# A four-layer attention and expert kernel: first tile ahead of the output folding, two more narrow-expert buffers, an early fold

## The chip, the cores and the metric

The kernel runs on one core of a Trainium2 chip. The metric is device microseconds (us) of one execution, median over runs. Matrix products run on TensorE (PE; its weight loads are shown as PEld), elementwise work on VectorE (DVE) and ScalarE (ACT), indexed transfers and a few powers on GpSimd (POOL). SyncE (SP) issues most of the transfers (DMAs). Each engine runs its own list of instructions in order and waits on semaphores.

## The reference

`x` is a (2, 1024, 256) fp32 tensor and `ctx` holds 77 keys a batch. Four layers follow each other, each a cross attention and a feed-forward block, each with layernorm and a residual sum:

```python
# layer 0 attention, 16 heads of 64 on 16-wide slices of the input, 77 keys, key mask
scores = einsum('bhqe,bhke->bhqk', Q, K) / 8
attn = softmax(where(mask, -1e9, scores))
out = einsum('bhqk,bhkv->bqhv', attn, V).reshape(Bq, Sq, -1) @ Wo.T + bo
# layer 0 feed-forward: 64 experts of hidden width 192, 8 of them a token, at most 128 rows an expert
x_buf = zeros((E * C + 1, 256)).at[idx].set(x[tok])
h = silu(einsum('ecd,edf->ecf', xb, w_gate)) * einsum('ecd,edf->ecf', xb, w_up)
y = einsum('ecf,efd->ecd', h, w_down)          # weighted, summed by token, plus a shared expert
# layer 2 feed-forward: 8 experts of width 1024 with gelu, 2 a token; layer 3 attention: 16 heads, 77 keys
```

Layer 1 (a second attention and a local attention with its feed-forward) and the last expert block are not touched.

## The kernel before, in words

The stages run one after the other: `a0` (first attention), `m0` (narrow experts), `a1`, local attention, `a2`, `m2` (`halved_experts`, the third block), `a3` (`fourth_attention`), `m3`. A stage's buffers are opened in its own scope; what must outlive a stage, or be there ahead of it, sits in an `Ahead` object.

**First attention, `low_rank_attention` (L796).** Tokens are taken in 16 tiles of 128. Because there are only 77 keys, the query weights are multiplied into the keys ahead of the tiles (`fold`, 16 small products, each copied out), and the output weights are multiplied into the value weights (`wp`). The function `outputs` (L1320) does the latter: 8 fp32 products give one bias row (`rows_made`, L1324), 8 more give `wp` in two halves (`wp_made`, L1327); DVE's `split_bo` adds `bo`, splits the row into three bf16 parts, and copies `wp` out (`wp_copied`). The parts go to DRAM and come back as three rows `bo3`, which each `project` adds by a bf16 product with ones. Then, for every tile: `turn` (transpose the normalised tile), `score` in three groups, DVE's `mask` and `maximum`, ACT's exponential, `turn_p` (transpose the probabilities, 10 pieces), `value`, DVE's `invert` and `unload`, `turn_o`, `project`, DVE's `add`, which gives the new `x` of the tile; then its router logits, its ranks among experts, and its slots (`place_slot`, L1136).

The order on each engine is written out by hand as cycles: in cycle c, PE does `turn_p(c)`, `turn(c+2)`, `score(c+1)`, `value(c)`, `turn_o(c)`, `project(c)`, and DVE works on add(c-1), mask(c+1), norm(c+3), invert(c) and so on. Cycle −1 is the start: the scores of tile 0, and behind them `outputs`. The layernorm statistics of the tiles (`stats_pair`, two tiles a pair) are spread over the first cycles by `STAT_PAIRS`; in a cycle they stand behind `norm` and ahead of `invert`. POOL raises the variances of a pair to the power −1/2 (`power_x`), and of each new tile, and scatters the rows of a tile to the experts' slots: 8 indirect DMAs a tile, 128 in all (L941), 7 a cycle and the rest at the end.

SP loads the inputs, then fills the slots with zeros in 16 transfers, half of them ahead of its wait for the split bias row and half behind; then the shared expert's weights, zeros for the sums, the first four gate-and-up weights, and, when every scatter is done, the first row loads.

**Narrow experts, `narrow_experts` (L2359).** 32 pairs of experts. Buffers: four for rows (`xb`), four for gate-and-up weights (`wgu`, 768 KB a pair), six for down weights (`wd`, 384 KB). SP's loop issues, for each pair q from 4 on, the rows, which wait until pair q−4's rows are transposed (`turned`) and its row numbers found (`found`), then the gate-and-up and the down weights, each when its buffer is free:

```python
for q in range(NG):
    load_d(q)
for q in range(NG, npair):
    load_x(q)
    load_gu(q)
    load_d(q)
```

**Third block, `halved_experts` (L2798).** 16 passes (two an expert). `every_step` runs phases with lags: on PE the row transposition and first product of a pass, then its second product (`down`) one step later and the back-transposition of the result (`back`, in two parts) two steps later; DVE copies it out weighted (`copy_y`), POOL scatter-adds it to the sums (L2846).

**Fourth attention, `fourth_attention` (L323).** SP loads the first tiles of `x`, the first batch's fold (1,232 KB), the bias parts `c3` and the values, once the stage has begun.

## Time and profile before

| | |
|---|---|
| time, median of 3 runs | 2244.62 us (2235.33 to 2250.46) |
| the profiled execution: its own time, its span | 2244.4 us, 2242.6 us |
| mean granted PE clock | 0.951 |
| busy share: PE, PEld, DVE, ACT, POOL | 91%, 68%, 49%, 42%, 27% |
| DMA over the span | 255.35 MB, mean 114 GB/s |
| narrow experts: PE's first instruction | 257.30 |
| fourth attention: SP's first load | 1737.52 |

The rows are of one profiled execution, times in us from the start of the span. A timeline line is a run of like instructions on one engine: its start, the us they took, the code line, output and input by the program's names, shapes, and how many (x10). In brackets stands the idle time of that engine just ahead of it and what ended it. SPq is SP's DMA issue. The clock is a share of full speed: 1.00 is 2.4 GHz, 0.50 is 1.2 GHz.

### The profile page before, as it was taken

Reading aid. Unit: us, or ns where it says so; the run is one execution under the profiler, and the core shown is the slowest. Engines: PE = TensorE matmul, PEld = TensorE weight load, DVE = VectorE, ACT = ScalarE, POOL = GpSimd, SP = SyncE. Lnnn points to the kernel's source line nnn. Section 1 sums busy time; section 2 is a strip of 40 time slices with the busy share of each in tenths; the row PEclk is TensorE's granted clock in tenths of the full one; section 3 lists DMA queues with packets and bytes.
Section 4 is the critical chain, followed back from the end, with each engine's and each line's share of the span. In section 5 each row is a group of like instructions: output and inputs, shape, how many; then the busy total and the mean of one; then the engine's idle time right before and its main releaser. Section 6 shows DMA issues by size and latency. Waiting matters only on the chain. (4 is left out here: it accounts for less than half of the span.)

```text
span 2242.6 us, 39355 instructions
## 1 busy us (share of the span) xinstructions
PE 2048.1 (91%) x12889; PEld 1530.6 (68%) x12889; DVE 1099.0 (49%) x4126; ACT 935.7 (42%) x2965; POOL 614.7 (27%) x553
## 2 busy tenths in 40 slices
PE   7999899785999899799989979879998899699999
PEld 4676577563666555466655568768886577599998
DVE  4776244475777632577754358721221565411221
ACT  3565122253777521377752135422222566333332
POOL 0677466421222100122210002222223122212212
PEclk9999899887999999999999979989999999799999
DMA  7600599875900110100000091111121910466662
GB/s 280 251 17 30 164 341 342 237 278 169 374 14 11 39 33 0 40 11 11 11 11 0 1 332 43 41 43 28 35 34 15 302 39 35 152 196 175 183 183 56
DMA packets 162510, 255.35 MB, mean 114 GB/s; under 512 B 37484, under 2 KB 125967, under 8 KB 161270
## 3 DMA queue, kind: packets, MB, share of 16 engines
q1 hardware_dynamic: 132886, 224.62, 28.7%
q0 software_dynamic: 29424, 28.21, 7.1%
q8 instruction: 107, 1.75, 0.3%
q14 instruction: 93, 0.76, 0.1%
HBM read 165.95 MB, written 101.04 MB: 119 GB/s over the span
## 5 line engine op out<-in xcount | busy, mean ns | idle before, releaser
L2752 ACT ACTIVATE m3e_ht<-m3e_h_bank,m3w_b 128x128 f32<-128x128 f32 x312 | 88.9, 368 | 191.9 <-PE m3e_h_bank L2724 191.9
L3360 ACT ACTIVATE la_probs<-la_probs,la_nb,la_invnorm 128x256 f32<-128x256 f32 x256 | 150.2, 594 | 0.0
L2735 PE MATMUL m3e_y_bank<-m3w_w,m3e_ht 128*128 x624 | 141.0, 380 | 0.0
L941 POOL DMA_INDIRECT m_xbuf<-m0w_rows,m0w_slots x128 | 127.2, 993 | 40.3 <-issue 36.9
L2906 ACT ACTIVATE m2e_ht<-m2e_h_bank,m2w_b 128x270 f32<-128x270 f32 x128 | 62.2, 486 | 179.3 <-PE m2e_h_bank L2871 179.2
L2699 POOL DMA_INDIRECT out<-m3e_y,m3e_dest x39 | 60.4, 1548 | 238.2 <-DVE m3e_y L2787 224.3
L2735 PEld LDWEIGHTS m3e_y_bank<-m3w_w,m3e_ht 128*128 128x128 f32 x624 | 115.8, 190 | 14.0
L2846 POOL DMA_INDIRECT m_sum<-m2e_y,m2e_dest x48 | 70.2, 1462 | 197.7 <-DVE m2e_y L2954 187.0
L2764 DVE COPY m3e_xt<-m3e_turned_bank 128x256 f32<-128x256 f32 x39 | 16.6, 425 | 217.1 <-PE m3e_turned_bank L2712 217.1
L2871 PE MATMUL m2e_h_bank<-m2e_xt,m2w_w 128*128 128x270 f32 x512 | 121.7, 396 | 0.0
L2443 POOL DMA_INDIRECT m_sum<-m0e_y,m0e_dest x64 | 98.8, 1544 | 82.6 <-DVE m0e_y L2615 57.1
L2881 PE MATMUL m2e_y_bank<-m2e_ht,m2w_w 128*128 128x270 f32 x512 | 119.2, 391 | 0.0
L2871 PEld LDWEIGHTS m2e_h_bank<-m2e_xt,m2w_w 128*128 128x128 f32 x512 | 97.2, 192 | 19.0
L3190 POOL COPY la_spread<-la_inv 128x512 f32<-128x512 f32 x32 | 19.5, 610 | 325.6 <-DVE la_inv L3282 325.6
L2881 PEld LDWEIGHTS m2e_y_bank<-m2e_ht,m2w_w 128*128 128x128 f32 x512 | 96.1, 190 | 18.2
L3185 POOL TENSOR_TENSOR la_invnorm<-la_clamped,all_minushalf 128x16 f32<-128x16 f32 x32 | 92.8, 2901 | 36.4 <-DVE la_clamped L3254 36.4
L3271 DVE CUSTOM_DVE_ANT_0 la_probs<-la_score_bank,lo_shut 128x256 f32<-128x256 f32 x256 | 98.0, 420 | 6.7 <-PE la_score_bank L3456 6.6
L2468 PE MATMUL m0e_gu_bank<-m0e_xt,m0w_wgu 128*128 128x128 f32 x768 | 93.2, 279 | 0.0
L2724 PE MATMUL m3e_h_bank<-m3e_xt,m3w_w 128*128 128x128 f32 x768 | 91.0, 278 | 0.2 <-DVE m3e_xt L2764 0.2
L2468 PEld LDWEIGHTS m0e_gu_bank<-m0e_xt,m0w_wgu 128*128 128x128 f32 x768 | 90.4, 196 | 0.6 <-issue 0.6
L2724 PEld LDWEIGHTS m3e_h_bank<-m3e_xt,m3w_w 128*128 128x128 f32 x768 | 88.9, 194 | 0.6 <-DVE m3e_xt L2764 0.6
L3647 PE MATMUL lf_g_bank<-lf_zt,lo_w 128*128 128x512 f32 x160 | 79.6, 622 | 7.7 <-DVEq L3565 7.7
(505 smaller groups left out, 4767.0 us busy)
## 6 DMA issues: line engine op xcount, KB each, us to landing
m3w_w<-in_m_w SPq DMA_DIRECT2D x32, 1024.0 KB, 6.6
m0w_wgu<-in_m_gu SPq DMA_DIRECT2D x32, 768.0 KB, 10.2
m_xbuf<-all_zeros SPq DMA_DIRECT2D x38, 528.0 KB, 5.9
m2w_w<-in_m_w SPq DMA_DIRECT2D x16, 1024.0 KB, 12.4
m3e_w<-in_m_w SPq DMA_DIRECT2D x15, 1024.0 KB, 5.9
m0e_wd<-in_m_down SPq DMA_DIRECT2D x32, 384.0 KB, 11.2
m_xbuf<-all_zeros SPq DMA_DIRECT2D x16, 576.0 KB, 7.3
m0w_xb<-m_xbuf SPq DMA_DIRECT2D x32, 288.0 KB, 8.0
```

Of the source, the lines that this page charges most:

```text
L941: nc.gpsimd.indirect_dma_start(k.slot_buffers[m.name][0][:, :], bass.IndirectOffsetOnAxis(ahead.slots[:, t, i:i + 1], 0), ahead.rows[t % R ...
L2443: nc.gpsimd.indirect_dma_start(sums[j][:, :], bass.IndirectOffsetOnAxis(dest[q % NY][:, i:i + 1], 0), y[q % NY][:, i, :], None, bounds_che ...
L2468: last = nc.tensor.matmul(gu_ps[u][:, i * 512 + j * P:i * 512 + (j + 1) * P], wgu[q % NG][:, i * DC + c, j * P:(j + 1) * P], xt[u][:, c, i ...
L2724: last = nc.tensor.matmul(h_ps[t % 2][half][:, i * R:(i + 1) * R], w1[t % NW][:, c, f0:f0 + P], xt[t % 2][:, c, :], start=c == 0, stop=c = ...
L2735: last = nc.tensor.matmul(y_ps[t % 2][0:R, 0:D], h_t[t % 2][:, c, :], ahead.w2[:, bass.ts(e, 1), c, :].rearrange("p o f -> p (o f)"), star ...
L2752: last = nc.scalar.activation(h_t[t % 2][:, 4 * half + i, :], h_ps[t % 2][half][:, i * R:(i + 1) * R], m.act, bias=ahead.b1[:, bass.ds(e * ...
L2871: last = nc.tensor.matmul(h_ps[n % 3][:, 0:N], ahead.w1[:, h // 2, c, f * P:(f + 1) * P], xt[h % 2][:, c, :], start=c == 0, stop=c == DC - 1)
L2881: last = nc.tensor.matmul(y_ps[c][:, 0:N], ahead.w2[:, h // 2, f, c * P:(c + 1) * P], h_t[h % 2][:, f, :], start=f == 0, stop=f == HC - 1)
L3185: nc.gpsimd.tensor_tensor(inv_norm[t % 2][:, :], clamped[t % 2][:, :], k.minus_half[:, :], ALU.pow).then_inc(powered.sem, 1)
L3271: last = nc.vector.tensor_tensor_reduce(probs[u][:, hh, :], score_ps[j][:, i * 2 * P:(i + 1) * 2 * P], lo.shut[:, int(t % TB == 0), :], 1. ...
L3360: last = nc.scalar.activation(probs[u][:, hh, :], probs[u][:, hh, :], ACT.Exp, bias=nb[u][:, hh:hh + 1], scale=inv_norm[u][:, hh:hh + 1], ...
L3647: last = nc.tensor.matmul(ps[:, :], w1[:, dc, i, :], z_t[g % 2][:, dc, :], start=dc == 0, stop=dc == DC - 1)
```

## The change

- **First attention.** PE's `outputs` is cut into `output_row` and `output_fold`. They leave cycle −1: in cycle 0, the row comes behind `turn_p(0)` and the fold behind `score(1, 0)`. The fold uses the first of the three `pt` banks and waits until its earlier content has been copied; `turn_p(1)` and `project(0)` wait for the fold's copy. On DVE, the row's and the fold's copies are steps of cycle 0, and the split of the row comes at the end of it. `project` of tiles 0 and 1 adds the bias by one fp32 row instead of the three bf16 rows. The statistics stand ahead of `mask` in their cycle, and one pair moves from cycle 1 to cycle 2. SP issues all 16 zero fills ahead of its wait for the split row.
- **Narrow experts.** `wgu` has six buffers: the last two lie in the memory of the first attention's `fold` and `values`. `wd` becomes lasting, and the first attention's weights (`wo`, `wq`, `wv`, `wk`, `bq`) lie in its memory. During the first attention, SP waits until those weights are used up and loads six down weights; it loads gate-and-up 4 after the last score and 5 after the last values product. The stage's own loop then loads only rows for pairs 4 and 5, and rows and weights from pair 6.
- **Third block and fourth attention.** The first fold and `c3` get buffers of their own, loaded by SP at the end of the third block's loads. In its last step, the second part of `back(14)` goes into the middle of `down(15)`, and DVE's copy of it ahead of `evict(15)`.

The diff, cut (the new fold's uses in `fourth_attention` are left out):

```diff
@@ -228,8 +228,14 @@
+            gu = 2 * DC * 2 * m.hidden
+            self.under = [s.sb("under0", [P, 16 * B * J]), s.sb("under1", [P, B * len(PROB_CHUNKS) * WIDE])]
             self.wgu = [s.sb(f"wgu{i}", [P, 2 * DC, 2 * m.hidden]) for i in range(4)]
+            self.wgu += [u[:, 0:gu].rearrange("p (c f) -> p c f", c=2 * DC) for u in self.under]
             self.wgu_in = s.lasting_sems("wguin", len(self.wgu))
+            self.down = s.sb("down", [P, 6, 3, D])
+            self.wd = [self.down[:, i, :, :] for i in range(6)]
+            self.wd_in = s.lasting_sems("wdin", len(self.wd))
@@ -266,6 +272,10 @@
+    def load_down(self, sp, q):
+        n = len(self.wd)
+        sp.dma_start(self.wd[q % n], self.d["down"][q]).then_inc(self.wd_in[q % n], 16)
@@ -298,6 +308,22 @@
+class FoldAhead:
+    def __init__(self, k):
...
+        s = Scope(k, self.ctx, "a3w")
+        self.fold = self.ctx.enter_context(k.nc.sbuf_tensor("a3w_fold0", [P, 16, DC, J], F32, side="right"))
+        self.c3 = self.ctx.enter_context(k.nc.sbuf_tensor("a3w_c3", [3, D], BF16, side="right"))
+        self.fold_in, self.c3_in = s.lasting_sems("in")
+    def load(self, sp, src):
+        sp.dma_start(self.fold[:, :, :, :], src.fold[:, 0]).then_inc(self.fold_in, 16)
+        sp.dma_start(self.c3[:, :], src.parts).then_inc(self.c3_in, 16)
@@ -334,7 +360,7 @@
         s = Scope(k, ctx, "a3")
-        fold, vw, c3 = s.sb("fold", [P, B, 16, DC, J]), s.sb("vw", [P, B, NC, D]), s.sb("c3", [3, D], BF16)
+        fold, vw, c3 = [k.fold_ahead.fold, s.sb("fold1", [P, 16, DC, J])], s.sb("vw", [P, B, NC, D]), k.fold_ahead.c3
@@ -381,9 +407,6 @@
-                def load_fold(b):
-                    sp.dma_start(fold[:, b, :, :, :], src.fold[:, b]).then_inc(fold_in[b], 16)
                 def load_vw(b):
@@ -391,13 +414,11 @@
                     sp.dma_start(k.x[:, t, :], k.m2_sum[t * P:(t + 1) * P, :]).then_inc(sem, 16)
-                load_fold(0)
                 load_x(1)
-                sp.dma_start(c3[:, :], src.parts).then_inc(c3_in, 16)
                 load_vw(0)
                     load_x(p)
-                load_fold(1)
+                sp.dma_start(fold[1][:, :, :, :], src.fold[:, 1]).then_inc(fold_in[1], 16)
                 ahead.load_router(sp)
@@ -790,7 +812,7 @@
 PER_CYCLE = 7
-STAT_PAIRS = {0: (2, 3), 1: (4, 5, 6), 2: (7,)}
+STAT_PAIRS = {0: (2, 3), 1: (4, 5), 2: (6, 7)}
@@ -804,13 +826,17 @@
         s = Scope(k, ctx, name)
-        fold, values = s.sb("fold", [P, 16, B, J]), s.sb("values", [P, B, len(PROB_CHUNKS), WIDE])
+        fold = ahead.under[0][:, :].rearrange("p (h b j) -> p h b j", h=16, b=B)
+        values = ahead.under[1][:, :].rearrange("p (b c w) -> p b c w", b=B, c=len(PROB_CHUNKS))
-        wk, bk, bks, bv = s.sb("wk", [P, DC, P]), s.sb("bk", [P, 8]), s.sb("bks", [P, 8]), s.sb("bv", [P, 8])
-        wq, wv, bq = s.sb("wq", [P, 8, P]), s.sb("wv", [P, 8, P]), s.sb("bq", [P, 8, 16])
-        wo, bo, kt = s.sb("wo", [P, 8, D]), s.sb("bo", [1, D]), s.sb("kt", [P, 8, B * J])
+        down = ahead.down[:, :, :, :].rearrange("p i r d -> p (i r d)")
+        wo, wq = down[:, 0:8 * D].rearrange("p (i d) -> p i d", i=8), down[:, 8 * D:12 * D].rearrange("p (i n) -> p i n", i=8)
+        wv, wk = down[:, 12 * D:16 * D].rearrange("p (i n) -> p i n", i=8), down[:, 16 * D:17 * D].rearrange("p (c n) -> p c n", c=DC)
+        bq = down[:, 17 * D:17 * D + P].rearrange("p (i n) -> p i n", i=8)
+        bk, bks, bv = s.sb("bk", [P, 8]), s.sb("bks", [P, 8]), s.sb("bv", [P, 8])
+        bo, kt = s.sb("bo", [1, D]), s.sb("kt", [P, 8, B * J])
@@ -895,23 +921,31 @@
-                for i in range(pieces // 2):
+                for i in range(pieces):
                     zero_slots(i)
                 sp.dma_start(bo3[:, :], bo_dram).then_inc(bo_in, 16)
-                for i in range(pieces // 2, pieces):
-                    zero_slots(i)
                 sp.dma_start(wgu[:, :, :], md["sgu"].rearrange("(c p) f -> p c f", p=P)).then_inc(shared_in, 16)
                         sp.dma_start(total[c * 512:(c + 1) * 512, :].rearrange("(p a) d -> p (a d)", p=P), k.zeros[:, 0:4 * D]).then_inc(ahead.sum_zeroed, 16)
-                for q in range(len(ahead.wgu)):
+                for q in range(4):
                     ahead.load_gate_up(sp, q)
+                sp.wait_ge(kt_made, 8)
+                sp.wait_ge(fold_made, 16)
+                sp.wait_ge(rows_made, 2)
+                sp.wait_ge(wp_made, 1)
+                for q in range(len(ahead.wd)):
+                    ahead.load_down(sp, q)
+                sp.wait_ge(scored, NG * T)
+                ahead.load_gate_up(sp, 4)
+                sp.wait_ge(valued, T)
+                ahead.load_gate_up(sp, 5)
                 ahead.wait_scattered(sp)
@@ -979,17 +1013,21 @@
-                def split_bo():
+                def copy_output_row():
                     dve.wait_ge(rows_made, 2)
                     nc.vector.tensor_tensor(brow[0][:, :], bo[:, :], out_ps[0:1, D:2 * D], ALU.add).then_inc(rows_copied, 1)
+                def copy_output_fold():
+                    dve.wait_ge(wp_made, 1)
+                    nc.vector.tensor_copy(wp[:, :, :].rearrange("p c d -> p (c d)"), pt_ps[0][:, :]).then_inc(wp_copied, 1)
+                def split_bo():
                     dve.wait_ge(rows_copied, 3)
                     then(nc.vector.tensor_copy(bpart[2][:, :], brow[1][:, :]))
-                    dve.wait_ge(wp_made, 1)
-                    nc.vector.tensor_copy(wp[:, :, :].rearrange("p c d -> p (c d)"), pt_ps[1][:, :]).then_inc(wp_copied, 1)
@@ -1163,24 +1201,28 @@
                     at(c - 2, place)
+                    for p in STAT_PAIRS.get(c, ()):
+                        stats_pair(p)
                     at(c + 1, mask, 0)
                     at(c + 1, maximum, 0)
+                    if c == 0:
+                        copy_output_row()
+                        copy_output_fold()
                     at(c + 1, mask, 1)
                         maximum(0, 2)
-                        split_bo()
                         stats_pair(1)
                     at(c + 3, norm)
-                    for p in STAT_PAIRS.get(c, ()):
-                        stats_pair(p)
                     at(c, invert)
                         at(c + 1, maximum, 2)
+                    if c == 0:
+                        split_bo()
                     at(c - 1, log)
@@ -1317,14 +1359,17 @@
-                def outputs():
+                def output_row():
                     pe.wait_ge(wo_in, 64)
                     last.then_inc(rows_made, 1)
+                def output_fold():
+                    pe.wait_ge(p_copied, 1)
                     for i in range(8):
-                        last = nc.tensor.matmul(pt_ps[1][:, i // 4 * D:(i // 4 + 1) * D], wv[:, i, :], wo[:, i, :], start=i % 4 == 0, stop=i % 4 == 3)
+                        last = nc.tensor.matmul(pt_ps[0][:, i // 4 * D:(i // 4 + 1) * D], wv[:, i, :], wo[:, i, :], start=i % 4 == 0, stop=i % 4 == 3)
                     last.then_inc(wp_made, 1)
@@ -1358,7 +1403,7 @@
                 def turn_p(t):
-                    if t == 0:
+                    if t == 1:
                         pe.wait_ge(wp_copied, 1)
@@ -1400,12 +1445,17 @@
                     if t == 0:
+                        pe.wait_ge(wp_copied, 1)
+                    if t == 2:
                         pe.wait_ge(bo_in, 16)
                         pe.wait_ge(added, t)
-                    nc.tensor.matmul(pt_ps[2][:, D:2 * D], k.ones3[:, :], bo3[:, :], start=True, stop=False)
+                    if t < 2:
+                        nc.tensor.matmul(pt_ps[2][:, D:2 * D], k.ones[0:1, :], brow[0][:, :], start=True, stop=False)
+                    else:
+                        nc.tensor.matmul(pt_ps[2][:, D:2 * D], k.ones3[:, :], bo3[:, :], start=True, stop=False)
                     for c in range(DC):
@@ -1469,13 +1519,16 @@
                     at(c, turn_p)
+                    if c == 0:
+                        output_row()
                     at(c + 2, turn)
                     at(c + 1, score, 0)
+                    if c == 0:
+                        output_fold()
                     at(c + 1, score, 1)
                         score(0, 2)
-                        outputs()
                     at(c, value)
@@ -2364,12 +2417,12 @@
     npair = m.ntiles // 2
-    NX, NG, ND = len(r.ahead.xb), len(r.ahead.wgu), 6
+    NX, NG, ND = len(r.ahead.xb), len(r.ahead.wgu), len(r.ahead.wd)
     with ExitStack() as ctx:
         wgu, wgu_in = r.ahead.wgu, r.ahead.wgu_in
-        wd = [s.sb(f"wd{i}", [P, 3, D]) for i in range(ND)]
+        wd, wd_in = r.ahead.wd, r.ahead.wd_in
         gate, gate_rest = s.pair("gate", [P, 2, P]), s.pair("gaterest", [P, P])
@@ -2416,16 +2468,15 @@
                 def load_d(q):
+                    sp.wait_ge(y_made, q - ND + 1)
+                    r.ahead.load_down(sp, q)
+                for q in range(NX, npair):
+                    load_x(q)
+                    if q >= NG:
+                        load_gu(q)
                     if q >= ND:
-                        sp.wait_ge(y_made, q - ND + 1)
-                    sp.dma_start(wd[q % ND][:, :, :], d["down"][q]).then_inc(wd_in[q % ND], 16)
-                for q in range(NG):
-                    load_d(q)
-                for q in range(NG, npair):
-                    load_x(q)
-                    load_gu(q)
-                    load_d(q)
+                        load_d(q)
                 sp.wait_ge(r.ahead.x_stored, 16 * (T // 2))
@@ -2815,6 +2866,8 @@
         BACK = [(0, 2), (2, 3)]
+        if k.attention_after_m2:
+            k.fold_ahead = FoldAhead(k)
@@ -2831,6 +2884,8 @@
                 every_step(NH, (0, load))
+                if k.attention_after_m2:
+                    k.fold_ahead.load(sp, k.folded["a3"])
@@ -2876,6 +2931,8 @@
                     for f in range(HC):
+                        if f == HC // 2 and h == NH - 1:
+                            back(h - 1, 1)
                         pe.wait_ge(acted, HC * h + f + 1)
@@ -2892,7 +2949,8 @@
-                every_step(NH, (0, turn), (1, up), (2, lambda h: back(h, 0)), (1, down), (2, lambda h: back(h, 1)))
+                every_step(NH, (0, turn), (1, up), (2, lambda h: back(h, 0)), (1, down),
+                           (2, lambda h: None if h == NH - 2 else back(h, 1)))
@@ -2953,7 +3011,13 @@
-                every_step(NH, (0, copy_x), (0, pick), (2, lambda h: copy_y(h, 0)), (1, evict), (0, weigh), (2, lambda h: copy_y(h, 1)))
+                def evict_behind(h):
+                    if h == NH - 1:
+                        copy_y(h - 1, 1)
+                    evict(h)
+                every_step(NH, (0, copy_x), (0, pick), (2, lambda h: copy_y(h, 0)), (1, evict_behind), (0, weigh),
+                           (2, lambda h: None if h == NH - 2 else copy_y(h, 1)))
         r.old_sems.close()
```

## Rows read from the trace of the kernel before

**Rows 1.** Timeline of PE and ACT, first tile: start, us, instruction group [idle before <- what ended it]
```profile
27.76 2.34 ACT L1238 ACTIVATE a_probs<-a_score_bank,a_mx 128x77 f32<-128x77 f32 x10 [0.83 <-DVE a_mx L1027]
...
27.99 3.61 PE L1324 MATMUL a_out_bank<-a_wo,a_bv 128*1 128x256 f32 x16
...
31.54 3.72 PE L1327 MATMUL a_pt_bank<-a_wo,a_wv 128*128 128x256 f32 x16
...
36.11 1.31 PE L1371 MATMUL a_pt_bank<-all_ident,a_probs 128*128 128x128 f32 x10 [0.85 <-DVE a_wp L992]
...
38.81 0.44 PE L1337 MATMUL a_turned_bank<-all_ident,a_xn 128*128 128x128 f32 x2 [1.40 <-DVE a_xn L1010]
...
42.00 2.47 PE L1388 MATMUL a_out_bank<-a_values,a_probst 128*128 128x96 f32 x20
```

**Rows 2.** Timeline of DVE and PE, first four cycles of the first attention
```profile
43.42 0.42 DVE L996 BATCH_NORM_STATS2 all_stats<-all_x 128x6 f32<-128x256 f32 x1
...
46.38 0.25 DVE L1033 RECIPROCAL a_inv<-a_out_bank 128x16 f32<-128x16 f32 x1
...
50.24 0.42 DVE L1044 TENSOR_TENSOR all_x<-all_x,a_pt_bank 128x256 f32<-128x256 f32 x1 [2.25 <-PE a_pt_bank L1410]
...
61.96 0.58 PE L1398 MATMUL a_turned_bank<-all_ident,a_o 128*128 128x128 f32 x2 [3.18 <-DVE a_o L1039]
...
77.85 0.42 DVE L1044 TENSOR_TENSOR all_x<-all_x,a_pt_bank 128x256 f32<-128x256 f32 x1 [0.33 <-PE a_pt_bank L1410]
...
80.72 0.65 DVE L1019 COPY_PREDICATED a_score_bank<-a_drop,a_masked 128x462 f32<-128x462 uint8 x1
...
87.85 0.42 DVE L1044 TENSOR_TENSOR all_x<-all_x,a_pt_bank 128x256 f32<-128x256 f32 x1
...
90.58 0.16 DVE L1136 TENSOR_SCALAR m0w_slots<-a_last 128x8 uint32<-128x8 f32 x1
```

**Rows 3.** The page's groups (POOL's scatters); timeline of POOL and SP's queue
```profile
L941 POOL DMA_INDIRECT m_xbuf<-m0w_rows,m0w_slots x128 | 127.2, 993 | 40.3 <-issue 36.9
...
70.81 1.19 POOL L941 DMA_INDIRECT m_xbuf<-m0w_rows,m0w_slots  x1 [3.17 <-DVE m0w_slots L1136]
...
246.76 0.97 POOL L941 DMA_INDIRECT m_xbuf<-m0w_rows,m0w_slots  x1 [0.30 <-issue]
...
249.08 1.91 SPq L263 DMA_DIRECT2D m0w_xb<-m_xbuf  x4
```

**Rows 4.** Windows: us, PE, PEld, DVE, ACT, POOL busy, PE clock, DMA share, GB/s
```profile
24.00:28.00 4.00, 4.00 (x10) 1.69 (x10) 2.58 (x4) 1.64 (x8) 0.00 (x0) 0.50 1.05 347
...
36.00:40.00 4.00, 2.50 (x15) 1.64 (x15) 1.80 (x8) 1.76 (x5) 0.70 (x1) 1.00 1.03 422
...
62.00:66.00 4.00, 4.00 (x14) 3.19 (x15) 2.13 (x10) 1.34 (x5) 0.06 (x1) 0.52 1.03 421
...
300.00:320.00 20.00, 19.51 (x149) 16.45 (x148) 8.53 (x40) 6.04 (x17) 12.31 (x8) 1.00 1.10 344
```

**Rows 5.** Waits of PE, 262–425 us: us, count, longest
```profile
PE m0e_turned_bank L2456 <- DMA m0w_xb<-m_xbuf: 5.9, 13, 1.1
```

**Rows 6.** Timeline of SP's queue: row loads of the narrow experts
```profile
270.53 0.38 SPq L263 DMA_DIRECT2D m0w_xb<-m_xbuf  x1
...
294.35 0.38 SPq L263 DMA_DIRECT2D m0w_xb<-m_xbuf  x1
...
401.80 0.38 SPq L263 DMA_DIRECT2D m0w_xb<-m_xbuf  x1
```

**Rows 7.** Timeline of PE and POOL, end of third block, start of fourth attention
```profile
1728.34 0.61 PE L2892 MATMUL m2e_back_bank<-all_ident,m2e_yt 128*90 128x128 f32 x4 [1.26 <-DVE m2e_y L2954]
...
1729.01 1.46 POOL L2846 DMA_INDIRECT m_sum<-m2e_y,m2e_dest  x1 [4.78 <-DVE m2e_y L2954]
...
1734.31 1.46 POOL L2846 DMA_INDIRECT m_sum<-m2e_y,m2e_dest  x1 [0.30 <-issue]
...
1744.30 6.40 PE L683 MATMUL a_score_bank<-a_fold,a_xnt 128*128 128x462 f32 x12 [0.16 <-DMA a_fold<-a_dram_fold]
```

More of the change, by code:

```diff
@@ L298, in load_weights @@
                     sp.dma_start(self.w2[:, e, :, :], d["w2"][e].rearrange("(c p) f -> p c f", p=P)).then_inc(self.weights_in, 16)
+class FoldAhead:
+    def __init__(self, k):
+        self.ctx = ExitStack()
+        s = Scope(k, self.ctx, "a3w")
[5 more added lines that the diff above has]
+        sp.dma_start(self.c3[:, :], src.parts).then_inc(self.c3_in, 16)
 def x_statistics(nc, k, block):
@@ L356, in fourth_attention @@
         x_ps, logit_ps, pos_ps = turned_ps[:, 0:D], out_ps[:, D:D + E], score_ps[2][:, 448:448 + E]
-        x_in, x1_in, fold_in, vw_in, c3_in = s.sems("xin", NP), s.sem("x1in"), s.sems("foldin"), s.sems("vwin"), s.sem("c3in")
+        x_in, x1_in, fold_in, vw_in, c3_in = s.sems("xin", NP), s.sem("x1in"), [k.fold_ahead.fold_in, s.sem("foldin")], s.sems("vwin"), k.fold_ahead.c3_in
         started, restat, powered, normed, turned, copied, scored = (
@@ L682, in score @@
                     for c in range(DC):
-                        last = nc.tensor.matmul(heads(score_ps[g], h0, h1), xn_t[t % 2][:, c, :], fold[:, b, h0:h1, c, :],
+                        last = nc.tensor.matmul(heads(score_ps[g], h0, h1), xn_t[t % 2][:, c, :], fold[b][:, h0:h1, c, :],
                                                 start=c == 0, stop=c == DC - 1, skip_group_check=True)
@@ L749, in fourth_attention @@
         old.close()
+    k.fold_ahead.ctx.close()
 class Experts:
@@ L2379, in narrow_experts @@
         gu_ps = [s.bank(f"gu{u}", 1024) for u in range(2)]
-        wd_in = s.sems("wdin", ND)
         sums, summed = r.ahead.sums, r.ahead.summed
```

## The prediction

> **What bounds the kernel now.** I read the page by engine first: TensorE (PE) is the busy engine almost everywhere, so a gain has to be a stretch in which PE stands idle or runs below its clock, or in which something that isn't PE sets the end. I then looked only at the three places that the change touches.
>
> First attention, start. The timeline of its first tile shows PE going through the output products (3.61 us for the bias row, 3.72 for the fold) while ScalarE (ACT) is still in the first tile's exponentials, then waiting 0.85 us for VectorE's (DVE) copy of the fold and 1.40 us for a normalised tile [rows 1]. The DVE timeline shows where this goes: the statistics of four tiles start at 43.42 and the first reciprocal, which needs only the values product that ended at 44.47, stands behind them until 46.38 [rows 1, 2]. The reader should then compare distances between the `add` steps (tile 0 at 50.24, tile 2 at 77.85, tile 3 at 87.85): two cycles took 27.61 us, the next 10.00 [rows 2]. Part of this is the clock: it is 1.00 at 36–40 and 0.52 at 62–66, behind PE's wait of 3.18 us [rows 2, 4].
>
> First attention, end. GpSimd (POOL) issues 128 row scatters from 70.81 to 246.76, busy 127.2 us with 40.3 us of idle before them, of which 36.9 is its own issue; only 3.4 us is a wait for another engine [rows 3]. The narrow experts' row loads wait for the last scatter and issue at 249.08 [rows 3]. So this attention ends when POOL does: what reaches the end is how much sooner the scatters start and are fed, not PE's time.
>
> Narrow experts. At 300–320 PE is busy 19.51 of 20 us and the DMA engines show a share of 1.10 at 344 GB/s; PE's waits on row loads come to 5.9 us in all [rows 4, 5]. The row loads issue 23.82 us apart over five pairs early on (4.76 a pair), then 107.45 over 21 pairs (5.12) [rows 6]. The slowdown is worth 21 × 0.353 = 7.4 us.
>
> Third block's end. The last four scatter-adds start 1.77 us apart from 1729.01, after POOL waited 4.78 us for DVE, and PE's last back-transposition waited 1.26 us [rows 7]. In the fourth attention PE waits for the fold load 0.16 us [rows 7].
>
> **The change, part by part.** *A, first attention.* Removed from the front: nothing of PE's work, only its order. The exponentials end at 27.76 + 2.34 = 30.10; the probabilities' transposes (1.31) then end at 31.4. The row (3.61) goes behind them; the chain from the second transposition to the end of the values product took 44.47 − 38.81 = 5.66; the fold (3.72) is now inside it [rows 1]. Sum: 31.4 + 3.61 + 5.66 + 3.72 = 44.4, against 44.47. So the reordering alone gains nothing by the first values product: PE's idle 2.25 us is traded for its idle until 30.1. DVE's two new waits (row, fold) end near 35 and 41; behind them stand mask, maximum and the next norm of tile 1, which PE reaches after the fold anyway.
>
> What gains is the statistics block. It is 46.38 − 43.42 = 2.96 us for four tiles (0.74 each) [rows 2], moved ahead of the mask, in DVE's wait for PE. The reciprocal then starts at 44.5 instead of 46.38: −1.9. The two copies in the cycle and the five small steps of the split (estimate 0.3, since the add waits 2.25 us for PE anyway) give add(0) at 48.6. In cycle 1, 1.2 for the add and its own statistics (0.42 + 0.74), 2.96 for tiles 8–11, then mask to next add, in the steady cycle 87.85 − 80.72 = 7.13 [rows 2]: add(1) at 59.9. First slots 90.58 − 87.85 = 2.73 later, so a first scatter near 63 against 70.81. In cycle 2, the step from add to mask (80.72 − 77.85 = 2.87), 2.96 for the pair moved into it, and 7.13: add(2) at 72.9, against 77.85, that is −5.0. After that the 10.0 us cycle is unchanged; POOL starts some 7.8 sooner and is fed 5.0 sooner, and its end lies between the two. I take **−5.7**, nearer to the feed. Ends: −8.9, all of the 7.6 us by which the first cycles exceed two of 10.00, and the 1.9 ahead of them, less 0.6 for the split; and −1.3, if the clock falls in cycle 1 as now: seven us at 0.52 lose 3.4, and DVE's chain 1.0.
>
> Edits at nothing: all zero fills and the bias split go by the queue of SyncE (SP) earlier or later than before, but the third projection, first to need the split row, comes after 60, with the split near 49; six down loads are queued in SP behind the gate-and-up loads, and what stands behind SP's new waits is only row loads that wait for POOL until 249.08 anyway [rows 3]. If POOL were not the cover, SP's wait for the last values product would be what they wait for. The first two projections use one fp32 row in place of three bf16 rows; the nearest row is a 128x256 fp32 product at 3.72/8 = 0.47 us, twice, off the end's path.
>
> *B, narrow experts.* Leaves the stage: two gate-and-up (768 KB) and six down loads (384 KB), 3.93 MB, 11.4 us at 344 GB/s [rows 4]. But SP can't run ahead with it: a row load waits until its buffer is found and turned, four pairs back, so early on the queue idles, and only pairs 4 and 5 lose their weights' transfers in the stretch that queues. 2 × 0.353 = **−0.7** [rows 6]. Ends: −7.4 (the queue never forms) and 0; a loss is excluded, since no transfer, wait or instruction is added to the stage.
>
> *C, third block and fourth attention.* The joined back-transposition lets POOL use part of its 4.78 us wait for the scatter that now opens the last four: up to one 1.77 us step off the tail, less the transposition's 0.61 on PE that now stands in the last product [rows 7], 1.16; I take −0.7, since its copy on DVE now stands ahead of the last eviction too. The early fold removes the 0.16 us wait and no more, because PE reaches that product late by the normalisation. Together **−0.9**; ends −1.3 and +0.6 (POOL wins nothing and the 0.61 stays on the path).
>
> Sum: −5.7 − 0.7 − 0.9 = −7.3. The profiled execution took 2244.4 us (span 2242.6 and 1.8 around it), 0.2 below the median; 2244.4 − 7.3 = 2237.1, so **2237**.
>
> **The rivals.** *R1, the narrow experts become PE-bound.* The 3.93 MB that leave equal 11.4 us of transfers, more than the 7.4 us of slowdown. For: the share of 1.10 with PE waiting on rows alone. Against: SP's waits, above. B = −7.4, sum −14.0: 2230.4.
>
> *R2, the gain in the first attention stays small.* PE still meets a gap in cycle 1 and the clock falls as at 62–66 [rows 4]. A = −1.3, sum −2.9: 2241.5. For: DVE has the same work in the cycle. Against: the block no longer stands between the values product and the reciprocal.
>
> *R3, slower.* PE is now idle from 27.99 to 30.10 and then starts with transposes, where before products filled it; the clock was 0.50 at 24–28 [rows 4]. If this gap loses the rise, every us of PE work costs a second one until it comes: the 11 us from 31.4 to about 42.4 cost 11 more. A = −5.7 + 11 = +5.3, sum +3.7: 2248.1. It decides if the clock at 32–42 is near 0.5. Against it: at 36–40 PE was busy 2.50 of 4 us and the clock stayed at 1.00 [rows 4]. The Trainium skill, "TensorE: Matmul & The Clock Gate", section "Part 4: PE-mode transpose", says that transposes don't count as PE work for the full clock in the same way; by that rule R3 would be the likelier and the time about 2248. The 1.00 at 36–40, a stretch of transposes and waits, speaks against it here.
>
> *R4, the change doesn't do what it says.* For the fold this is in the forecast (0.16 us). If the joined tail also gives nothing, it is 0.7 more: 2238.
>
> **How the numbers follow.** Forecast with R4 0.57, R1 0.15, R2 0.18, R3 0.10. The forecast's own range is 2233 to 2241 (A from −8.9 to −3, C at its ends). To leave no more than two in ten out, the range reaches down to R1 with A and C at their upper ends, 2226, and up past R2, 2246, without R3. A measurement of this kernel can tell about 1% from no change: 22 us. Faster by over 1% (below 2222) needs R1 with A and C beyond their upper ends: 0.06. Slower by over 1% needs more than R3: 0.03. The rest, 0.91, is within 1%.
>
> **What would show it.** A: the first scatter near 63–64, the last at about 241, row loads near 243; the reciprocal of tile 0 behind the values product without statistics between; clock 1.00 throughout 32–70. B: 5.12 us a pair still from the ninth pair on, some 5 us of PE waits on rows; R1 would show 4.8. C: the last scatter-add's gap to PE's last transposition shorter by 0.7, no fold wait. I am wrong on A if the last scatter doesn't move with the first, and on the whole if the experts' stage, not its start, is what moved.

## The result, and the profile after

The changed kernel takes 2232.33 us, median of 4 runs (2231.40 to 2233.12), against 2244.93 for the kernel before, a ratio of 0.9949 (95% interval 0.9926 to 0.9973). A set is a group of kernels run on one chip; two later sets of the same kernel give 2232.61 (0.9955, 0.9938 to 0.9973) and 2232.10 (0.9960, 0.9945 to 0.9975), 9 to 10 us below the kernel before of their own sets. The forecast was 2237, within 2226 to 2246. The profiled execution took 2232.14 us with a span of 2230.4, 12.2 less than before. One execution of the kernel before, in a later set, took 3467.12 us at a mean clock of 0.552 and is left out of every ratio and spread here.

The timeline of the first attention, PE, ACT, DVE, POOL and SP's queue:

```profile
24.44 3.56 ACT L1280 ACTIVATE a_probs<-a_score_bank,a_mx 128x77 f32<-128x77 f32 x16 [2.37 <-DVE a_mx L1065]
...
27.19 0.66 PE L1416 MATMUL a_pt_bank<-all_ident,a_probs 128*128 128x128 f32 x4 [2.00 <-ACT a_probs L1280]
...
28.86 3.62 PE L1366 MATMUL a_out_bank<-m0w_down,a_bv 128*1 128x256 f32 x16
...
29.16 0.42 DVE L1034 BATCH_NORM_STATS2 all_stats<-all_x 128x6 f32<-128x256 f32 x1
...
33.97 3.61 PE L1372 MATMUL a_pt_bank<-m0w_down 128*128 128x256 f32 x16
...
34.17 0.65 DVE L1057 COPY_PREDICATED a_score_bank<-a_drop,a_masked 128x462 f32<-128x462 uint8 x1 [1.96 <-PE a_score_bank L1401]
...
39.04 2.47 PE L1433 MATMUL a_out_bank<-m0w_under,a_probst 128*128 128x96 f32 x20
...
41.55 0.26 DVE L1071 RECIPROCAL a_inv<-a_out_bank 128x16 f32<-128x16 f32 x1 [1.00 <-PE a_out_bank L1433]
...
45.26 0.42 DVE L1082 TENSOR_TENSOR all_x<-all_x,a_pt_bank 128x256 f32<-128x256 f32 x1
...
56.14 0.42 DVE L1082 TENSOR_TENSOR all_x<-all_x,a_pt_bank 128x256 f32<-128x256 f32 x1 [0.74 <-PE a_pt_bank L1460]
...
57.92 1.05 PE L1401 MATMUL a_score_bank<-m0w_under,a_xnt 128*128 128x462 f32 x2
...
60.01 1.19 POOL L975 DMA_INDIRECT m_xbuf<-m0w_rows,m0w_slots  x1 [1.88 <-DVE m0w_slots L1174]
...
61.90 0.64 DVE L1057 COPY_PREDICATED a_score_bank<-a_drop,a_masked 128x462 f32<-128x462 uint8 x1
...
64.20 0.44 PE L1468 MATMUL a_turned_bank<-all_ident,m0w_rows 128*128 128x128 f32 x2 [1.30 <-DVE m0w_rows L1100]
...
69.18 0.42 DVE L1082 TENSOR_TENSOR all_x<-all_x,a_pt_bank 128x256 f32<-128x256 f32 x1 [1.31 <-PE a_pt_bank L1460]
...
79.90 0.42 DVE L1082 TENSOR_TENSOR all_x<-all_x,a_pt_bank 128x256 f32<-128x256 f32 x1
...
238.86 0.97 POOL L975 DMA_INDIRECT m_xbuf<-m0w_rows,m0w_slots  x1 [0.30 <-issue]
...
241.16 1.91 SPq L269 DMA_DIRECT2D m0w_xb<-m_xbuf  x4
```

The statistics start at 29.16, behind PE's first output products, and the reciprocal starts 0.04 us after the values product has ended (39.04 + 2.47 = 41.51); before, 1.91 lay between [rows 1, 2]. Tile 3's add comes 7.95 us sooner (79.90 against 87.85), and the last scatter 7.90 sooner (238.86 against 246.76) [rows 2, 3].

Not all of the block lies in a wait of DVE. In cycle 0 it does: DVE still waits 1.96 us for scores behind it. In cycle 2 the scores are there at 58.97 (57.92 + 1.05), but the mask starts at 61.90, behind the block, without a wait; in cycle 1 it starts 1.68 us after the scores. What is gone is PE's wait for DVE's unload in cycle 1, 3.18 us before [rows 2]; in its place PE waits 1.30 us for DVE in cycle 2 (the row at 64.20).

The same stretches by windows as before [rows 4] (us, PE, PEld, DVE, ACT, POOL busy, clock, DMA share, GB/s), and the one wait of PE in the narrow experts [rows 5]:

```profile
24.00:28.00 4.00, 1.85 (x8) 0.81 (x7) 3.79 (x11) 3.56 (x17) 0.00 (x0) 1.00 1.02 305
36.00:40.00 4.00, 4.00 (x22) 2.75 (x21) 1.75 (x3) 0.93 (x5) 0.00 (x0) 1.00 1.03 424
62.00:66.00 4.00, 2.34 (x15) 1.40 (x14) 3.87 (x9) 2.61 (x12) 3.09 (x4) 1.00 1.03 400
300.00:320.00 20.00, 18.22 (x137) 15.16 (x136) 7.54 (x36) 5.47 (x15) 11.94 (x8) 1.00 1.10 343
```

```profile
PE m0e_turned_bank L2507 <- DMA m0w_xb<-m_xbuf: 7.1, 15, 1.5
```

The clock is 1.00 at 24–28 and at 62–66, where it was 0.50 and 0.52. The narrow experts look as before: share 1.10, 343 GB/s, PE waiting for rows. Where these experts' stage begins and ends, and the third block's end, on PE, POOL and SP (of before: PE's 257.30 in the table, [rows 6, 7]):

```profile
249.51 1.94 PE L2507 MATMUL m0e_turned_bank<-all_ident,m0w_xb 128*128 128x128 f32 x8 [4.74 <-PEq L890]
...
305.19 0.38 SPq L269 DMA_DIRECT2D m0w_xb<-m_xbuf  x1
...
392.76 0.38 SPq L269 DMA_DIRECT2D m0w_xb<-m_xbuf  x1
...
423.49 0.65 PE L2565 MATMUL m0e_gu_bank<-m0e_hbv,m0e_one 1*77 1x256 f32 x2
...
1716.03 0.64 PE L2949 MATMUL m2e_back_bank<-all_ident,m2e_yt 128*90 128x128 f32 x4 [1.00 <-DVE m2e_yt L3002]
...
1718.01 1.46 POOL L2901 DMA_INDIRECT m_sum<-m2e_y,m2e_dest  x1 [3.82 <-DVE m2e_y L3012]
...
1721.54 1.46 POOL L2901 DMA_INDIRECT m_sum<-m2e_y,m2e_dest  x1 [0.30 <-issue]
...
1731.16 6.82 PE L704 MATMUL a_score_bank<-a3w_fold,a_xnt 128*128 128x462 f32 x12
```

The same end of the experts' stage in the kernel before:

```profile
431.26 0.65 PE L2514 MATMUL m0e_gu_bank<-m0e_hbv,m0e_one 1*77 1x256 f32 x2
```

The experts' stage takes 174.63 us (249.51 to 424.14); before it took 174.61 (257.30 to 431.91). The row loads issue 4.76 us apart up to 305.19 and then, over 17 pairs up to 392.76, 5.15 us apart; before it was 5.12 over 21 pairs [rows 6]. Behind PE's wait of the third block, three scatter-adds follow in place of four. The fourth attention's scores no longer wait for the fold, but this first group takes 6.82 us where it took 6.40 [rows 7]. Counted from the end of the third block's last first-layer product it starts 1.08 us sooner and ends 0.66 sooner; the clock is 0.50 at 1729–1733 here, as it was at 1742–1746 before.

Where the 12.2 us are: 7.8 by PE's start in the narrow experts, 0.0 in them, 4.0 in the second attention (from its first transposition to the local attention's first score 107.5 us before, 103.5 after), 0.4 from the third block's last first-layer product to the last experts, less 0.2 given back there; the rest, about 0.3, lies between these stretches. The second attention is not touched by the change. The experiments say what part is the change's.

### The profile page after: what moved, and what is told of

Same layout as the page of the kernel before. It is cut to its first block and busy times, and to the rows that moved or that the text cites. A ratio compares the mean times of both kernels' runs of the same rounds, so it can differ in the third digit from the quotient of the medians.

```text
span 2230.4 us, 39362 instructions
## 1 busy us (share of the span) xinstructions
PE 2039.7 (91%) x12891; PEld 1524.3 (68%) x12891; DVE 1097.9 (49%) x4126; ACT 936.5 (42%) x2965; POOL 613.6 (28%) x553
## 5 line engine op out<-in xcount | busy, mean ns | idle before, releaser
L1280 ACT ACTIVATE a_probs<-a_score_bank,a_mx 128x77 f32<-128x77 f32 x256 | 62.0, 333 | 49.2 <-DVE a_mx L1065 48.5
L3639 DVE SCALAR_TENSOR_TENSOR lf_hidt<-lf_a_bank,lo_b,lf_gelu 128x512 f32<-128x512 f32 x40 | 30.0, 750 | 103.9 <-ACT lf_gelu L3690 103.7
```

## The experiments

**The kernel before, again** (no edit).

> The kernel before, unchanged, a second profile. Theory: where the PE clock falls is not set by the program alone. The half clock at 20-28 us and the 107.5 us of the second attention (first transposition 442.0 to the local attention's first score 549.5) may then come out otherwise here: the first tile's exponentials between 24.4 and 27.8 us, the second attention between 103 and 108 us, and the time anywhere in 2235 to 2250. Rival: both come from the order of the kernel before; then 27.8, 107.5 and about 2245 are seen again.

Measured: 2238.84 us (12 runs; 0.9994, 0.9979 to 1.0008), the profiled execution 2244.52. Windows of its first attention:

```profile
24.00:28.00 4.00, 4.00 (x18) 1.55 (x18) 2.47 (x5) 3.55 (x16) 0.00 (x0) 1.00 1.04 315
40.00:44.00 4.00, 4.00 (x16) 2.89 (x15) 2.85 (x9) 2.80 (x12) 0.00 (x0) 0.50 0.46 183
48.00:52.00 4.00, 3.49 (x12) 2.71 (x12) 1.59 (x5) 1.45 (x6) 0.00 (x0) 0.50 1.02 407
```

The same program had half clock at 24–28 in one execution and at 40–52 in the other. Tile 0's add came at 51.04 all the same (50.24 before), the last scatter at 246.18, and the second attention took 105.8 us. So early exponentials don't bring the gain by themselves: here the fall came later. The theory holds.

**Parts of the first attention put back.** In the first, the order:

```diff
-                    if c == 0:
-                        output_row()       # behind turn_p(0)
...
-                    if c == 0:
-                        output_fold()      # behind score(1, 0)
+                        output_row()       # c == -1, behind score(0, 2)
+                        output_fold()
```

with DVE's copies, the bf16 bias rows and half of the zero fills back in their places.

> The changed kernel with the order of the output products, the bias and the zero fills put back; the statistics stay ahead of the mask. Theory (the prediction's step): the statistics' place is what gains; add of tile 2 comes near 72 to 73, the last scatter near 241, total about 2234 to 2236. Rival: the order gains, the statistics little; add of tile 2 near 76 to 78, last scatter 245 to 247, total about 2238 to 2241.

Measured: 2230.31 us (0.9953, 0.9937 to 0.9968); tile 0's add at 44.83, tile 2's at 68.89, the last scatter at 238.81. As in the theory, and better than its numbers: without the order nothing is lost. In the second, the statistics, both their place and the pair moved between cycles:

```diff
-STAT_PAIRS = {0: (2, 3), 1: (4, 5), 2: (6, 7)}
+STAT_PAIRS = {0: (2, 3), 1: (4, 5, 6), 2: (7,)}
...
                     at(c + 3, norm)
+                    for p in STAT_PAIRS.get(c, ()):
+                        stats_pair(p)
                     at(c, invert)
```

> The changed kernel with the statistics put back behind the norm and one pair back in cycle 1; the order of the output products stays changed. Theory: without the statistics' move the gain of the first attention is mostly gone, the last scatter 244 to 247, total about 2237 to 2240. Rival: the order alone keeps it, last scatter near 239 to 241, total 2232 to 2235.

Measured: 2238.88 us (0.9989, 0.9977 to 1.0001). The timeline shows the first of the six tiles' statistics in cycle 1, the reciprocal behind them, and PE's wait for the unload; then windows of the same kernel:

```profile
54.16 0.42 DVE L1034 BATCH_NORM_STATS2 all_stats<-all_x 128x6 f32<-128x256 f32 x1
...
58.60 0.25 DVE L1071 RECIPROCAL a_inv<-a_out_bank 128x16 f32<-128x16 f32 x1
...
59.36 0.44 PE L1443 MATMUL a_turned_bank<-all_ident,a_o 128*128 128x128 f32 x2 [3.18 <-DVE a_o L1077]
...
63.51 0.42 DVE L1082 TENSOR_TENSOR all_x<-all_x,a_pt_bank 128x256 f32<-128x256 f32 x1 [2.19 <-PE a_pt_bank L1460]
```

```profile
56.00:60.00 4.00, 0.82 (x7) 0.65 (x6) 3.59 (x16) 0.46 (x3) 1.89 (x3) 1.00 0.99 394
62.00:66.00 4.00, 4.00 (x18) 3.54 (x16) 1.36 (x8) 1.37 (x4) 0.55 (x1) 0.50 1.03 413
```

While DVE does the block, PE is busy 0.82 of 4 us, and then runs at 0.50. The same wait and the half clock behind it are in both profiles of the kernel before (3.18 us in [rows 2], 3.17 in the second). The last scatter is at 244.73: of the 7.9 us, 5.9 are lost again. The theory holds.

**The statistics behind the reciprocal**, in the changed kernel:

```diff
-                    for p in STAT_PAIRS.get(c, ()):   # ahead of mask(c + 1, 0)
-                        stats_pair(p)
...
                         at(c + 1, maximum, 2)
...
+                    for p in STAT_PAIRS.get(c, ()):
+                        stats_pair(p)
```

> The changed kernel with the same statistics behind the reciprocal, the unload and the third mask of their cycle, in place of ahead of the first mask. Theory: what costs is only that the block stood between the values product and the reciprocal; behind it does as well as ahead: add of tile 0 near 45 to 46, the last scatter 237 to 240, total 2230 to 2236. Rival: the block has to lie in the time in which VectorE waits for scores; behind the reciprocal it delays the next add by up to 3 us a cycle and PE's clock falls: add of tile 2 at 72 or later, the last scatter 242 to 246, total 2236 to 2241.

Measured: 2246.27 us (1.0016, 0.9998 to 1.0034), no gain at all. DVE's timeline, with PE's wait for tile 0's add, and a window:

```profile
50.03 0.42 DVE L1034 BATCH_NORM_STATS2 all_stats<-all_x 128x6 f32<-128x256 f32 x1
...
50.77 0.41 DVE L1082 TENSOR_TENSOR all_x<-all_x,a_pt_bank 128x256 f32<-128x256 f32 x1
...
51.33 0.41 PE L1416 MATMUL a_pt_bank<-all_ident,a_probs 128*128 128x128 f32 x2 [2.91 <-DVE all_x L1082]
```

```profile
56.00:60.00 4.00, 4.00 (x19) 3.71 (x19) 1.83 (x4) 1.39 (x6) 0.00 (x0) 0.50 0.97 378
```

The last scatter is at 251.95 and tile 2's add at 81.52, both later than the rival's numbers. The theory falls and the rival's mechanism holds: a block that no longer delays the reciprocal delays the add, PE waits 2.91 us for that, and runs at half clock from 53 to 69. Of the 13.1 us to the first profile's last scatter, 2.5 were lost ahead of the block: the clock fell at 22–25 and 29–32 too, and the first reciprocal came at 44.10. So of the three places the one ahead of the mask is the cheapest. It is not free: the cycles to the adds of tiles 1 and 2 take 10.88 and 12.08 us at full clock, and those without statistics 10.00.

**The statistics' move alone**, on the kernel before (the two edits of `STAT_PAIRS` and its place), in two sets:

> The kernel before with one edit: the statistics of a cycle ahead of its mask, and one pair moved from cycle 1 to cycle 2. Theory: this is all of the first attention's gain; add of tile 0 near 45, the last scatter 237 to 240, total 8 us below the kernel before, 2232 to 2235. Rival: it needs the new order of the output products or the early weights with it; then add of tile 0 is near 47 to 50, the last scatter 242 to 246, total within 4 us of the kernel before.

> The kernel before with the statistics' move alone, again, beside the changed kernel on one chip. Theory: the 2240.0 of its first set is a draw of the clock, and its profile (last scatter 239.90) tells the truth; here it comes within 3 us of the changed kernel, some 7 below the kernel before. Rival: the statistics alone leave the start open to a fall of the clock, which the other parts of the change prevent in most executions; then it is again 5 to 8 us slower than the changed kernel, and a profile of a slower execution has half clock between 40 and 52 us and add of tile 0 near 50.

Measured: 2240.03 us (0.9983, 0.9968 to 0.9999) and 2235.37 (0.9982, 0.9966 to 0.9998), beside 2232.10 for the changed kernel in the second set. The profiles' last scatters are at 239.90 and 243.37; the first is of the fastest of its 12 executions (2232.43). Windows of the second profile, and DVE's timeline:

```profile
24.00:28.00 4.00, 4.00 (x10) 1.78 (x10) 2.65 (x5) 2.09 (x10) 0.00 (x0) 0.50 1.04 314
40.00:44.00 4.00, 4.00 (x10) 1.58 (x10) 3.69 (x14) 0.37 (x1) 1.72 (x2) 0.61 0.60 243
```

```profile
47.15 0.26 DVE L1033 RECIPROCAL a_inv<-a_out_bank 128x16 f32<-128x16 f32 x1 [1.00 <-PE a_out_bank L1388]
...
50.23 0.42 DVE L1044 TENSOR_TENSOR all_x<-all_x,a_pt_bank 128x256 f32<-128x256 f32 x1 [1.13 <-PE a_pt_bank L1410]
```

The reciprocal stands right behind the values product here too; what is late is PE, at half clock. From tile 0's add on, the cycles are as in the changed kernel or nearly (10.46 to tile 1 against 10.88). So the statistics alone bring at least part of the gain: 4.2 and 6.7 us below the kernel before, and 3.3 us less than the changed kernel in the set that has both; the intervals of the two ratios, 0.9982 and 0.9960 (0.9945 to 0.9975), overlap. The first set's theory (2232 to 2235) is missed; of the second's numbers "some 7 below" is met and "within 3 us" just missed. Clock at 24–28 was low in three of the five profiles whose products stand in the old order, and below 1.00 in two of the nine with the new one (0.83 there); PE's instructions are the same up to that point, so these runs can't settle whether the order keeps the clock up or the draws were kind.

**Four buffers again** in the narrow experts (all edits of that part put back: `wgu` of four, `load_d` in the stage's own loop).

> The changed kernel with four gate-and-up buffers and the down weights loaded in the narrow experts' stage, as before. Theory: the two pairs of weights fetched early are worth nothing, the stage stays at 169.7 us from PE's first transposition to its last value fold (257.30 to 426.97 before, 249.51 to 419.19 after) within 1 us, total 2232 within 2. Rival: the early weights gain several us that another loss hides; then the stage is 3 us longer or more here.

Measured: 2233.76 us (0.9969, 0.9958 to 0.9980); the stage takes 173.27 us to its last product (168.3 to the theory's end), PE waits 5.9 us for rows. In the three profiles of the changed kernel it took 174.63, 173.75 and 172.87. Over all profiles the mean is 174.9 of five with four buffers (173.27 to 176.42) and 174.0 of eight with six (172.87 to 174.64). By these means the early weights are worth about 1 us, which the spread of the single profiles covers; the total comes from a set without the changed kernel and can't say more.

**Light weights in the narrow experts:**

```diff
                     sp.wait_ge(gu_made, q - NG + 1)
-                    r.ahead.load_gate_up(sp, q)
+                    sp.dma_start(wgu[q % NG][:, 0, 0:16], d["gu"][q][:, 0, 0:16]).then_inc(wgu_in[q % NG], 16)
```

> In the narrow experts the gate-and-up loads of pairs 6 to 31 are cut to 16 columns of one chunk, so most of these weights are wrong and 26 transfers of 768 KB are gone. Theory (the prediction's bound): transfers slow the stage by about 7 us; PE's waits on rows go, all pairs run at 4.76 us, the stage from PE's first transposition to its end takes 167 to 169 us in place of 174.6. Rival: the row waits come from the order in SP's queue, not from the amount; then the stage stays above 173.

Measured (one run): 2224.79 us, the stage 165.66.

```profile
300.00:320.00 20.00, 20.00 (x152) 16.76 (x150) 8.58 (x40) 6.81 (x19) 13.06 (x9) 1.00 0.93 204
```

PE is busy 20.00 of 20 us and no longer waits for rows; the row loads issue 4.76 us apart to the end. The transfers do slow this stage, by 7.2 to 9.0 us against the three profiles of the changed kernel (my bound was 7.4); fetching the weights of two pairs early doesn't relieve it.

**The third block's end and the fold put back** (`back(14, 1)` behind `down(15)`, its copy behind the eviction, fold and `c3` loaded by the fourth attention):

> The changed kernel with the joined back-transposition and the early fold put back as before. Theory: from the third block's last first-layer product (1706.7 after, 1718.7 before) to the fourth attention's first scores takes 25.6 us as before, 1.0 more than the 24.5 with the change; total 1 us more than the changed kernel. Rival: the fold's place gains nothing and the join alone was hidden by the barrier: 24.5 again.

Measured: 2232.50 us (0.9958, 0.9942 to 0.9974), not to be told from the changed kernel's 2232.61 in the same set. By the profile, from the start of the last first-layer product to the fourth attention's scores it takes 25.36 us (1704.4 to 1729.76), with four scatter-adds in the tail, of which POOL's timeline shows the first and the last, and PE's the scores:

```profile
1714.63 1.46 POOL L2901 DMA_INDIRECT m_sum<-m2e_y,m2e_dest  x1 [4.78 <-DVE m2e_y L3009]
...
1719.92 1.46 POOL L2901 DMA_INDIRECT m_sum<-m2e_y,m2e_dest  x1 [0.30 <-issue]
...
1729.76 5.94 PE L706 MATMUL a_score_bank<-a3w_fold,a_xnt 128*128 128x462 f32 x12
```

That stands against 24.46, 24.45 and 24.45 in the changed kernel's profiles: 0.9 us, as the theory has it. But the score group takes 5.94 here and 6.82 in the first of those, so that the next group starts equally late (33.92 and 33.91 us from the same point; 33.8 and 33.4 in the two later profiles of the changed kernel); by the last experts' first product 0.5 is left (235.3 against 234.7 to 234.8).

**The changed kernel, again**, twice:

> The changed kernel, unchanged, a second profile, on the chip of the next runs. Theory: the 12 us between the two first profiles are about 8 of the first attention, 1 of the third block's end and 3 to 4 of clock that falls by chance in the second attention; so the last scatter again near 237 to 240, the second attention 103 to 106 us, total 2230 to 2236. Rival: all 12 belong to the change; then 2232 and 103.5 us again.

> The changed kernel beside the run before. Theory: 9 us below the kernel before, as in its other sets (ratio 0.995 to 0.996), the last scatter 237 to 239, the second attention 102 to 106 us. Rival: its gain is a matter of the chip or the hour; then the ratio is 0.998 here, as the statistics alone had.

Measured: 2232.61 and 2232.10 us. The last scatter is at 237.27 and 237.25, the second attention takes 102.3 and 103.9. In both, the clock is 1.00 from 20 to 76 us, and tile 2's add comes at 68.31 and 68.29: the 238.86 of the first profile had a fall at 64–72. The second text's theory holds (10.0 us below). The first text's theory and rival aren't parted: 2232.61 us and about 102 to 104 in the second attention are what the rival said as well.

**Idle products in PE's gaps**, to keep the clock up where a stage begins (`y_ps[0]` is not yet in use there; the same at six other places):

```diff
             def _(pe):
+                for _ in range(16):
+                    nc.tensor.matmul(y_ps[0][:, 0:P], k.ident[:, :], k.ident[:, :], start=True, stop=True)
                 pe.wait_ge(ahead.weights_in, 16 * ahead.weights_n)
```

> The changed kernel with idle products (identity times identity, 128x128 fp32, results unused) put into PE's idle time at seven stage boundaries: 6 at the first attention's end, 14 at the second attention's start, 6 at the local attention's, 14 at the third attention's, 6 at the third block's, 9 at the fourth attention's, 16 at the last experts'. Theory: the stages lose 1.5 to 3 us each because their first products run at half clock (score group 6.8 us at the fourth attention's start, 4.6 for the next one); with the clock kept up the total falls 6 to 12 us below the changed kernel, to 2221 to 2227. Rival: those first products wait for other engines anyway; the total stays within 2 us, or rises where the idle products overrun the gap.

Measured: 2231.36 us (6 runs, 2225.60 to 2238.95; 0.9946, 0.9929 to 0.9963): no gain that can be told against the 2232.61 of the same set, so the rival holds. The profile is of the slowest of the six. In the last experts it does what it should, clock 1.00 at 1949–1953, where their products begin at 1949.67. In the fourth attention, windows and the score group:

```profile
1734.00:1738.00 4.00, 2.30 (x13) 1.90 (x12) 2.41 (x9) 0.37 (x1) 1.11 (x2) 0.82 0.98 314
1738.00:1742.00 4.00, 4.00 (x8) 1.90 (x9) 1.57 (x5) 0.37 (x1) 0.54 (x1) 0.61 1.12 362
```

```profile
1738.17 6.02 PE L706 MATMUL a_score_bank<-a3w_fold,a_xnt 128*128 128x462 f32 x12
```

The clock is 0.82 over 1734–1738, where PE waits 1.31 us between the two transpositions, and 0.61 behind. The group takes 6.02 us, not the 4.63 of the next group at full clock; without idle products it takes 5.50 to 6.95 in the other profiles, so no gain is shown here.

## Why the prediction was right or wrong

The range held the time and the sign was right; the forecast moved 7.3 us where 9 to 12.6 were measured. The step that was mis-sized is A, −5.7 on the record: the last scatter moved by 7.9, and by 9.5 in the two profiles without a fall of the clock (246.76 to 237.25), a little past the end of −8.9.

*The first values product at 44.4.* It ended at 41.51. The sum took the exponentials' end of 30.10 from a profile in which the clock was 0.50 at 24–28 [rows 4]; they ended at 28.0. These 2.1 us are most of the 2.9 by which this term was off, and the adds of tiles 0 to 2 came 3.3 to 3.8 us sooner than the sum had them. The change isn't needed for that: in the second profile of the kernel before the exponentials end at 28.0 too. The order itself is worth nothing, as the step said: with the old order and the clock up, tile 0's add comes at 44.83, with the new at 45.20 to 45.49.

*The statistics.* Right that they are what gains: with them alone put back 5.9 of 7.9 us are lost. The step said that they go into DVE's wait for PE. That holds in cycle 0; in cycles 1 and 2 the block delays the mask, and the two cycles are 2.96 us longer than two of 10.00 (the sum had them 4.3 longer, for it added the block in full). Moved behind the reciprocal, the block delays the add instead and costs more. In all three profiles with the statistics in their old place half clock follows PE's wait of 3.2 us, and no profile with that place has full clock there, so how much of the 5.9 is the block and how much the clock can't be parted.

*The cycles.* Add to add I had 11.3 and 13.0; measured 10.88 and 13.04, and 12.1 for the second at full clock. The distances were right; the start and the clock made the rest.

*POOL.* I set its end between its own start (−7.8) and the feed (−5.0). The feed decides: tile 3's add moved by 7.95, the last scatter by 7.90, though the first scatter moved by 10.8. In all fourteen profiles the last scatter starts 158.83 to 159.05 us behind tile 3's add.

*B, −0.7 between −7.4 and 0.* The stage took 174.63 against 174.61 us in the first pair, and with four buffers 173.27 lies between the changed kernel's three values. Zero or −0.7 can't be told apart. R1 is out: behind 305.19 the pairs still go at 5.15 us, and at 4.76 only where the transfers are cut. Two pairs' worth of weights fetched early shortens the queue at its beginning and not its pace.

*C, −0.9.* 0.9 by the scores' start and 0.5 by the last experts' first product (0.7 between the means of the five profiles without it and of the changed kernel's three). The fold is worth nothing: where it is loaded late, PE waits 0.16 us for it in one of the five profiles and not at all in four. The scores' earlier start is partly given back, since the first group then takes longer (6.82 us against 5.94).

*R2* is out by the clock at 62–66. *R3* is out in the changed kernel's profiles: PE waited 2.00 us for the exponentials and began with transpositions, and the clock stayed at 1.00 from 24 to 64. The trace disagrees with the rule of the Trainium skill ("TensorE: Matmul & The Clock Gate", "Part 4: PE-mode transpose") as I had applied it: the ten transposition passes at 27.19 and 28.06 took 0.66 and 0.88 us at full clock, behind that gap. Seven of the nine profiles with this order show the same. In the other two (idle products, statistics behind) the clock had already been 0.50 at 22–25, and fell to 0.50 again at 29–32, behind the gap; the first values product then ended 2.6 us later, not 11.

*The second attention's 4.0 us* were in no step. Windows of it, 8 us apart as its start is, before and after:

```profile
460.00:470.00 10.00, 7.94 (x49) 5.28 (x49) 8.62 (x38) 4.93 (x19) 2.83 (x7) 0.92 1.04 379
470.00:480.00 10.00, 9.57 (x61) 7.49 (x62) 7.48 (x27) 5.81 (x21) 2.28 (x4) 0.74 0.56 184
```

```profile
452.00:462.00 10.00, 7.28 (x49) 4.93 (x49) 8.58 (x39) 4.89 (x19) 3.16 (x6) 1.00 1.01 370
462.00:472.00 10.00, 9.20 (x79) 7.17 (x80) 9.58 (x39) 6.27 (x25) 3.28 (x6) 1.00 0.63 204
```

The clock is 0.92 and 0.74 in the one and 1.00 in the other. The stage took 107.5 and 105.8 us in the two profiles of the kernel before, 103.5, 102.3 and 103.9 in the changed kernel's, 104.4 and 103.7 with the statistics' move alone, and between 100.4 (light weights) and 108.3 (idle products) in the others. So a stage that no edit touches was slower in both profiles of the kernel before than in all others but one; that it was a draw is not shown, and neither is a way from the change to it. The totals don't settle it. The last scatter's mean over the profiles is 246.47 before and 237.79 after, 8.7 us, and 0.5 to 0.7 for C makes 9.2 to 9.4, where the two later sets show 9.1 and 10.0 and the first 12.6; but of the two profiled executions of the kernel before one lies 5.7 us above the median of its runs, and the changed kernel's lie 0.2 to 5.9 below theirs.

## What to carry to other kernels

Work that another engine doesn't wait for yet belongs where its engine waits anyway, or, where there is no such wait, ahead of the consumer that loses least by it. Here the statistics of twelve tiles in three cycles cost 5.9 us more ahead of the reciprocal than ahead of the mask, and 13.1 more behind the reciprocal (2.5 of them lost earlier), by the last scatter of one profile each and with what the clock lost. Even ahead of the mask they lengthen two cycles by 2.96 us together. Where a stage's end is set by a queue that is fed tile by tile, price the feed of the tiles, not the queue's start. And before a gain of a few us is given to an edit, profile the unchanged program a second time.

## What was not expected of the hardware

One program shows half clock at 24–28 us in one execution and at 40–52 in another, with nearly the same end (last scatter at 246.76 and 246.18); the runs of the kernel before spread over 2232 to 2252 us, those of the changed kernel over 2225 to 2238. And 26 smaller loads took the DMA share from 1.10 only to 0.93, while the bytes fell from 343 to 204 GB/s.
